# Two-layer decoder on one core: last four chunks and last norm by pairs of blocks, narrower waits, new step orders

## The reference

```
x = layernorm(x + L0_attn(x))    # linear attention, 16 heads, elu + 1
x = layernorm(x + L0_xattn(x))   # 4 experts of token ids: silu(x C) * (x C), times C
x = layernorm(x + L0_ffn(x))     # 8 dense experts, width 256, weights from a sigmoid router, top 2 as a fallback
x = layernorm(x + L1_attn(x))    # 16 heads in groups of 32 tokens, half the heads rolled by 16
x = layernorm(x + L1_xattn(x))   # softmax(x C^T / 16) C under a padding mask
x = layernorm(x + L1_ffn(x))     # 8 experts of width 176, softmax router, top 2, and a shared expert of width 352
# an expert: (silu(x Wg^T) * (x Wu^T)) Wd^T, times its weight
```

## Time and profile before

| | us |
|---|---|
| median of 3 runs | 455.77 (455.28 to 457.13) |
| the profiled execution | 452.04 |
| its span, first to last instruction | 450.2 |
| PE busy / weight loads | 424.8 / 365.9 |
| DVE / ACT / POOL busy | 250.6 / 247.2 / 261.9 |
| transfers | 35.2 MB, 24% of 16 engines' span |

### The profile page before, as it was taken

One profiled execution on the slowest core, in us unless ns is written; L12 is line 12 of the kernel. 1 busy time (PEld: TensorE's weight loads), 2 busy tenths in 40 slices (PEclk: granted clock), 3 DMA queues, 4 the chain that ended last, 5 costly groups with the idle time before them and its releaser, 6 DMA issues.

```text
span 450.2 us, 9291 instructions
## 1 busy us (share of the span) xinstructions
PE 424.8 (94%) x3668; PEld 365.9 (81%) x3668; DVE 250.6 (56%) x627; ACT 247.2 (55%) x424; POOL 261.9 (58%) x217
## 2 busy tenths in 40 slices
PE   7999999999999999999999997799999999999992
PEld 5788889997887887788888986588888888888981
DVE  5568557668437935565354757347435566533233
ACT  4747664773783446518337674454526756565331
POOL 1242753646774897548674663665547574877661
PEclk9999999999999999999999999999999999999996
DMA  8334200021221423312232021232041221433101
GB/s 253 121 92 169 70 1 0 2 70 49 75 90 48 139 75 99 131 49 80 66 95 66 8 76 41 87 85 81 6 149 42 82 81 48 159 126 128 41 1 47
DMA packets 15671, 35.22 MB, mean 78 GB/s; under 512 B 2027, under 2 KB 5995, under 8 KB 15628
## 3 DMA queue, kind: packets, MB, share of 16 engines
q1 hardware_dynamic: 15152, 34.00, 24.1%
q10 hardware_dynamic: 476, 0.63, 0.5%
HBM read 33.05 MB, written 1.05 MB: 76 GB/s over the span
## 4 chain that ended last, share of the span: by engine, by line
PE 50%; DVE 5%; ACT 4%; POOL 4%; issue 2%; DMA 1%; SPq 1%; ACTq 0%; POOLq 0%; DVEq 0%
PE bank L435 9%; PE bank L438 8%; PE bank L436 8%; PE bank L679 5%; PE bank L681 5%; PE bank L680 5%; ACT x_tok L905 2%; DVE stats L1303 2%; PE bank L753 2%; POOL rstd L1158 1%; PE bank L741 1%; DMA state<-o_tok 1%; PE bank L725 1%; PE bank L636 1%; PE bank L727 1%
## 5 line engine op out<-in xcount | busy, mean ns | idle before, releaser
L1192 POOL TENSOR_TENSOR h_lo<-hraw,h_hi 128x512 fp32r<-128x512 f32 x76 | 98.2, 1296 | 60.2 <-ACT h_hi L993 60.0
L435 PE MATMUL bank<-xT_hi,pk_hi 128*128 128x512 f32 x256 | 103.3, 404 | 4.1 <-DVE hraw L1480 3.2
L436 PE MATMUL bank<-xT_hi,pk_lo 128*128 128x512 f32 x256 | 101.6, 397 | 0.7 <-issue 0.7
L993 ACT ACTIVATE h_hi<-hraw 128x512 fp32r<-128x512 f32 x76 | 47.9, 630 | 81.7 <-DVE hraw L1480 75.0
L1198 POOL TENSOR_TENSOR pk_lo<-pk_raw,pk_hi 128x512 fp32r<-128x512 f32 (+1 forms) x44 | 74.7, 1697 | 17.2 <-ACT pk_hi L1011 17.0
L1480 DVE TENSOR_TENSOR hraw<-bank,sil 128x512 f32<-128x512 f32 x76 | 52.3, 688 | 53.7 <-PE bank L438 21.0
L438 PE MATMUL bank<-xT_lo,pk_hi 128*128 128x512 f32 x256 | 80.8, 397 | 0.0
L679 PE MATMUL bank<-pk_hi,h_hi 128*128 128x256 f32 x272 | 78.1, 287 | 2.1 <-DVE x_tok L1494 2.0
L681 PE MATMUL bank<-pk_hi,h_lo 128*128 128x256 f32 x272 | 76.9, 283 | 0.0
L680 PE MATMUL bank<-pk_lo,h_hi 128*128 128x256 f32 x272 | 76.8, 282 | 0.0
L1203 POOL TENSOR_TENSOR pk_lo<-pk_raw,pk_hi 128x256 fp32r<-128x256 f32 (+1 forms) x44 | 42.3, 962 | 34.4 <-ACT pk_hi L1022 34.4
(11 more groups left out here) (245 smaller groups left out, 727.0 us busy)
## 6 DMA issues: line engine op xcount, KB each, us to landing
pk_raw<-pk_f_dram SPq DMA_DIRECT2D x28, 448.0 KB, 3.4
pk_raw<-pk_f_dram SPq DMA_DIRECT2D x16, 512.0 KB, 3.5
pk_raw<-pk_f_dram SPq DMA_DIRECT2D x16, 256.0 KB, 2.7
kv_buf<-pk_x_dram SPq DMA_DIRECT2D x4, 512.0 KB, 3.5
x_tok<-x_rows_dram SPq DMA_DIRECT2D x1, 1024.0 KB, 9.5
pk_raw<-pk_x_dram SPq DMA_DIRECT2D x4, 256.0 KB, 6.4
out_dram<-x_tok SPq DMA_DIRECT2D x4, 256.0 KB, 2.2
kv_buf<-w_attn_dram SPq DMA_DIRECT2D x1, 768.0 KB, 4.4
```

What stands on the lines that cost most here:

```text
L435: pe.matmul(o, w(kc)[0], x(kc)[0], start=kc == 0, stop=False)
L436: pe.matmul(o, w(kc)[1], x(kc)[0], start=False, stop=False)
L993: A(h_hi[:, row, at * 512:(at + 1) * 512], hraw[:, s % 2, :], ACT.Copy).then_inc(sems["hid_hi"], 1)
L1192: pool.tensor_tensor(h_lo[:, row, q], hraw[:, s % 2, :], h_hi[:, row, q].bitcast(F32), ALU.subtract).then_inc(sems["hid_lo"], 1)
```

## The change

- The last four chunks go by pairs of blocks: step `e` is `down` for blocks 0 and 1, `f` for blocks 2 and 3; the order ends `e48 e49 e50 f48 e51 f49 f50 f51`.
- The last norm (11) goes by the same pairs: DVE `w0`, `w1` (addition and statistics of two tiles), POOL `w0`, `w1`, ACT tiles 4 to 6, and DVE tile 7 (`last_apply`); the last store waits for both.
- `gate(s)` for s = 18 to 48 waits for silu of s - 2 alone; the wait for `hid_mul >= s - 1` moves to `up(s)`, between the two products. `up` of an L1 chunk behind a shared chunk waits for silu of s - 2 (`up(49)`: for the multiplication of 46).
- `down(u)`, u below 24, waits for the additions by pairs: blocks 0 and 1 of the unit before ahead of its own blocks 0 and 1, then the others.
- All five orders are new. The diff is cut in the orders, where "..." stands for whole lines of a list, and leaves out the name of the new semaphore.

```diff
 SP_ORDER = """
-G0 D0 G1 D1 S0 G2 D2 G3 D3 G4 D4 G5 D5 G6 D6 G7 D7 G8 D8 G9 D9 G10 D10 G11 D11 S1 G12 S2 S3 D12 G13 D13 G14 D14 R0 G15
-D15 G16 G17 G18 G19 S4 G20 G21 G22 G23 G24 G25 G26 G27 R1 G28 G29 G30 G31 G32 G33 G34 G35 G36 G37 G38 G39 O0 G40 G41
-G42 G43
+G0 D0 G1 D1 S0 G2 S1 D2 G3 D3 G4 D4 G5 D5 G6 D6 G7 D7 G8 D8 G9 D9 G10 D10 G11 S2 S3 D11 G12 D12 G13 D13 G14 D14 R0 G15
+D15 G16 G17 G18 G19 G20 G21 G22 S4 G23 G24 G25 G26 G27 R1 G28 G29 G30 G31 G32 G33 G34 G35 G36 G37 G38 G39 G40 G41 G42
+G43 O0
 """.split()
 PE_ORDER = """
 b0.0 b0.1 b0.2 b0.3 b0.4 b0.5 b0.6 b0.7 b1.0 b0.8 b1.1 b0.9 b1.2 b1.3 b1.4 b1.5 b1.6 b1.7 n0.2 b1.8 g0 g1 b1.9 g2 g3
-d0 g4 n1.2 g5 g6 d1 g7 g8 d2 g9 g10 d3 g11 g12 d4 g13 r0.2 d5 g14 r0.3 g15 g16 u16 d6 g17 d7 u17 g18 u18 g19 u19 d8
-g20 u20 g21 u21 r1.2 d9 r1.3 g22 u22 g23 d10 u23 g24 u24 g25 u25 g26 u26 g27 d11 u27 d12 g28 u28 g29 d13 u29 g30 u30
-g31 u31 d14 d15 g32 u32 g33 u33 a0.2 g34 u34 a0.3 a0.4 d16 a0.5 a0.6 a0.7 g35 a0.8 u35 g36 u36 g37 u37 d17 a0.10 g38
-u38 a0.25 g39 u39 a0.11 d18 a0.26 g40 u40 g41 d19 u41 g42 u42 a0.14 g43 u43 a0.15 g44 d20 a0.16 u44 g45 a0.17 d21
-a0.18 u45 g46 u46 g47 u47 a0.21 d22 a0.22 d23 g48 u48 g49 u49 a1.2 g50 a0.24 a1.3 a1.4 u50 d24 a1.5 a1.6 a1.7 d25 a1.8
-g51 u51 g52 u52 g53 d26 a1.10 u53 a1.25 d27 d28 a1.11 d29 g54 a1.26 u54 g55 u55 g56 u56 g57 u57 a1.14 d30 d31 a1.15
-g58 u58 a1.16 g59 d32 a1.17 u59 a1.18 d33 d34 g60 u60 a1.21 g61 u61 a1.22 g62 u62 g63 d35 d36 d37 a1.24 u63 g64 d38
-u64 g65 d39 u65 g66 d40 u66 g67 u67 g68 d41 u68 g69 d42 d43 u69 g70 u70 g71 u71 g72 u72 d44 d45 d46 d47 g73 u73 g74
-u74 g75 u75 d48 d49 d50 d51
+d0 g4 n1.2 g5 g6 d1 g7 g8 d2 g9 d3 g10 g11 d4 r0.2 g12 g13 r0.3 g14 d5 g15 d6 g16 u16 g17 u17 g18 d7 u18 g19 u19 g20
+u20 g21 d8 u21 r1.2 d9 r1.3 g22 u22 g23 u23 g24 d10 u24 g25 u25 d11 g26 u26 g27 u27 g28 d12 u28 g29 u29 d13 g30 u30
+g31 u31 d14 d15 g32 u32 g33 u33 g34 a0.2 u34 g35 a0.3 a0.4 d16 a0.5 a0.6 a0.7 u35 a0.8 g36 u36 g37 u37 g38 u38 g39
+a0.10 d17 a0.25 d18 a0.11 u39 g40 a0.26 u40 g41 u41 g42 u42 g43 d19 a0.14 u43 a0.15 g44 d20 a0.16 u44 g45 a0.17 u45
+g46 a0.18 d21 u46 g47 u47 a0.21 d22 a0.22 d23 g48 u48 g49 u49 g50 u50 g51 a1.2 d24 d25 a0.24 a1.3 a1.4 d26 u51 a1.5
+a1.6 a1.7 g52 a1.8 d27 u52 g53 u53 g54 d28 a1.10 u54 a1.25 g55 a1.11 u55 a1.26 g56 u56 g57 u57 d29 d30 d31 a1.14 g58
+a1.15 u58 g59 a1.16 u59 g60 a1.17 u60 a1.18 d32 d33 d34 d35 a1.21 g61 u61 g62 a1.22 d36 u62 g63 u63 g64 u64 d37 a1.24
+g65 d38 d39 u65 g66 u66 g67 u67 g68 d40 d41 u68 d42 g69 u69 g70 u70 d43 d44 d45 d46 g71 u71 g72 u72 g73 u73 g74 u74
+g75 u75 d47 e48 e49 e50 f48 e51 f49 f50 f51
 """.split()
 ACT_ORDER = """
-p0 p1 b0.0 b0.1 b0.2 b0.3 p2 p3 p4 X0 X1 b0.8 X2 X3 b1.0 b1.1 b1.2 b1.3 n0.1 n0.2 b1.8 G0 D0 s0 h0 s1 h1 s2 h2 s3 n1.1
...
-a0.14 s42 h42 s43 a0.15 D14 a0.16 h43 s44 h44 a0.17 G15 D15 s45 h45 s46 a0.20 h46 s47 a0.21 h47 G16 D16 G17 D17 a0.22
...
-D34 h64 s65 G35 D35 G36 D36 h65 s66 h66 s67 G37 z0 h67 D37 G38 s68 h68 s69 D38 G39 D39 G40 h69 s70 h70 s71 h71 s72 h72
-D40 G41 D41 G42 D42 s73 G43 D43 h73 s74 h74 s75 h75 z1
+p0 p1 p2 b0.0 b0.1 b0.2 b0.3 p3 p4 b0.8 b1.0 b1.1 X0 X1 X2 X3 b1.2 b1.3 n0.1 n0.2 G0 b1.8 s0 h0 s1 h1 S0 s2 h2 s3 n1.1
...
+h41 s42 h42 s43 a0.15 a0.16 D14 G15 h43 s44 a0.17 h44 s45 h45 s46 D15 G16 a0.20 a0.21 h46 s47 h47 D16 G17 D17 G18
+a0.22 s48 D18 G19 S3 D19 G20 h48 s49 h49 s50 a1.1 a1.2 a0.24 h50 a1.4 S4 s51 D20 G21 D21 G22 D22 h51 s52 h52 a1.9 s53
...
+h64 s65 D34 G35 D35 h65 s66 G36 h66 s67 h67 D36 G37 D37 G38 s68 D38 h68 s69 h69 s70 h70 G39 D39 G40 D40 G41 D41 s71
+G42 D42 h71 s72 G43 h72 s73 z0 h73 s74 h74 s75 D43 h75 z1
 """.split()
 POOL_ORDER = """
-p1 p3 p4 X0 X1 X2 X3 n0.0 v0 G0 D0 l0 l1 n1.0 l2 l3 l4 l5 l6 l7 l8 l9 r0.0 l10 l11 l12 G1 D1 l13 l14 l15 l16 l17 G2
...
-G15 D15 a0.19 l45 l46 l47 G16 D16 G17 a1.0 S3 D17 G18 l48 S4 l49 D18 G19 D19 G20 D20 G21 a1.7 D21 a1.8 l50 l51 l52 l53
...
-l71 D40 G41 D41 G42 D42 G43 D43 l72 l73 l74 l75 y1
+p1 p3 p4 X0 X1 X2 n0.0 X3 v0 G0 l0 l1 n1.0 l2 S0 l3 l4 l5 l6 l7 l8 l9 r0.0 l10 l11 l12 D0 l13 G1 l14 l15 D1 G2 l16
...
+l44 l45 a0.19 D15 G16 l46 l47 D16 G17 D17 G18 D18 G19 a1.0 D19 l48 l49 G20 S3 l50 D20 G21 D21 G22 D22 l51 a1.7 a1.8
...
+G31 l60 l61 D31 G32 D32 G33 l62 l63 D33 G34 l64 D34 G35 D35 l65 G36 l66 D36 G37 D37 G38 D38 l67 l68 l69 l70 G39 D39
+G40 D40 G41 D41 y0 G42 D42 G43 l71 l72 l73 l74 D43 l75 w0 w1
 """.split()
 DVE_ORDER = """
-n1.0 m2 m3 a0 m4 n1.2 m5 m6 a1 m7 m8 a2 m9 m10 a3 r0.0 m11 a4 m12 r0.2 m13 a5 m14 r0.3 m15 r0.4 a6 m16 r0.5 m17 a7 m18
-r1.0 m19 a8 m20 r1.2 a9 m21 r1.3 m22 r1.4 a10 m23 m24 m25 r1.5 a11 m26 m27 a12 c m28 a13 m29 m30 m31 a14 a15 a0.0 m32
-a0.2 m33 a0.3 a0.4 a16 a0.5 a0.6 m34 a0.7 a0.8 m35 m36 a0.9 a0.10 m37 a17 a0.25 m38 m39 a0.11 a0.26 a18 m40 a0.12 m41
-a19 a0.14 m42 a0.15 a20 m43 a0.16 m44 a0.17 a21 a0.18 a0.19 m45 m46 m47 a0.21 a22 a0.22 a23 a0.23 a1.0 m48 a1.2 a1.3
...
-a1.14 o57 m57 a1.15 a1.16 o58 m58 a1.17 o59 m59 a1.18 a1.19 o60 m60 a1.21 o61 m61 a1.22 a1.23 m62 x0 m63 m64 y0 o65
-m65 o66 m66 o67 m67 o68 m68 o69 m69 o70 m70 o71 m71 o72 m72 o73 m73 o74 m74 o75 m75 x1 y1
+n1.0 m2 m3 a0 m4 m5 n1.2 m6 a1 m7 m8 a2 m9 a3 r0.0 m10 a4 m11 r0.2 m12 m13 r0.3 m14 a5 r0.4 m15 a6 r0.5 m16 a7 m17
+r1.0 m18 m19 m20 a8 m21 r1.2 a9 r1.3 m22 m23 r1.4 a10 m24 m25 a11 m26 r1.5 m27 a12 m28 c m29 a13 m30 m31 a14 a15 a0.0
+m32 a0.2 m33 a0.3 m34 a0.4 a0.5 a0.6 a0.7 m35 a0.8 m36 a16 a0.9 m37 m38 a17 a0.10 a0.25 a18 a0.11 m39 a0.26 m40 a0.12
+m41 a19 a0.14 m42 a0.15 m43 a20 a0.16 m44 a0.17 m45 a0.18 a0.19 a21 m46 a0.21 m47 a22 a0.22 a23 a0.23 m48 a1.0 m49 m50
...
+o57 m57 a1.14 a1.15 o58 m58 a1.16 o59 m59 a1.17 o60 m60 a1.18 a1.19 a1.21 o61 m61 a1.22 m62 a1.23 m63 x0 m64 o65 m65
+o66 m66 o67 m67 o68 m68 o69 m69 o70 m70 y0 o71 m71 o72 m72 o73 m73 o74 m74 o75 m75 w0 w1 z1
 """.split()
...
             def store(h):
                 for t in range(0, HT, 2):
                     T = HT * h + t
-                    sp.wait_ge(sems["ln_done"], 4 * (10 + h) + t + 2)
+                    if h and t:
+                        sp.wait_ge(sems["ln_done"], 4 * nth(11) + 3)
+                        sp.wait_ge(sems["last_done"], 1)
+                    else:
+                        sp.wait_ge(sems["ln_done"], 4 * (10 + h) + t + 2)
                     sp.dma_start(out_v[:, T:T + 2, :], x_tok[:, T:T + 2, :]).then_inc(sems["out_done"], 16)
 
             for step in SP_ORDER:
...
                 else:
                     pe.wait_ge(sems["g_lo"], 2 * E0 + u - U_F1 + 1)
                 first = {0: 0, 2 * EX: 1, S_F0: 2, S_F0 + 2 * E0: 3, S_F1: 8, S_F1 + N1: 9}.get(s)
-                if s >= 2:
+                if S_F0 + 2 <= s <= S_F1:
+                    pe.wait_ge(sems["silu_done"], s - 1)
+                elif s >= 2:
                     pe.wait_ge(sems["hid_mul"], s - 1)
                 if u < U_F1:
                     product(s, bank[2 * c][:, :], 0, D, c * P, first).then_inc(sems["gate_ready"], 1)
...
                 if u < U_F0:
                     return
                 if u < U_F1:
+                    pe.wait_ge(sems["hid_mul"], s - 1)
                     product(s, bank[2 * c + 1][:, :], KC * D, D, c * P).then_inc(sems["up_ready"], 1)
                     return
                 m, h = u - U_F1, (u - U_F1) // N1
...
                               cwT[:, h * 512:(h + 1) * 512], start=True, stop=True).then_inc(sems["cw_ready"], 1)
                 if m and routed(m - 1):
                     pe.wait_ge(sems["m1_done"], routed_no(m))
-                else:
-                    pe.wait_ge(sems["hid_mul"], s)
+                elif m == 1:
+                    pe.wait_ge(sems["hid_mul"], S_F1 - 1)
+                else:
+                    pe.wait_ge(sems["silu_done"], s if m == 0 else s - 1)
                 product(s, bank[(3 * m + 2) % 4][:, :], D, P, 0).then_inc(sems["up_ready"], 1)
 
             def open_sums(h):
...
                     pe.matmul(bank[4 + j][:, :], zero_r[:, 0:P], zero_r[:, :], start=True, stop=False,
                               skip_group_check=True)
 
-            def down(u):
+            def down(u, tiles=range(HT)):
                 if u < U_F0:
                     e = u % EX
                     chunks, wh, wl = KC, x0_pack(e, pk_hi, xp_hi), x0_pack(e, pk_lo, xp_lo)
...
                     pe.wait_ge(sems["d_lo"], 2 * E0 + m + 1)
                     chunks, wh, wl = 1, d_part("f1", m, pk_hi), d_part("f1", m, pk_lo)
                 pe.wait_ge(sems["hid_lo"], 2 * (u + 1) if u < U_F1 else S_F1 + u - U_F1 + 1)
-                if 1 <= u < U_F1:
-                    pe.wait_ge(sems["acc_done"], 4 * u)
                 closed = u < U_F1
-                for t in range(HT):
+                for t in tiles:
                     o = bank[4 + t // 2][:, (t % 2) * D:(t % 2 + 1) * D]
+                    if 1 <= u < U_F1 and t % 2 == 0:
+                        pe.wait_ge(sems["acc_done"], 4 * u - 2 + t)
                     for kc in range(chunks):
                         row, at = place(u, kc)
```

(61 more changed lines are left out.)

28 lines of the change are left out of this document (13 added, 15 removed).

## The result

The changed kernel takes 452.82 us (median of 8 executions, 448.86 to 455.45) against 455.52 (8 executions) for the kernel before: ratio 0.9937, with a 95% interval of 0.991 to 0.9963. Measured a second time it was 0.9955 (0.9926 to 0.9983). So it is faster by some 0.6%: 2.9 us by the ratio, 2.7 between the two medians. The forecast was 7.5 us: the sign is right, the size is too large by a factor of 2.6. The median lies just inside the stated range.

What follows compares the result with a forecast made beforehand. PE, busy for 94% of the span, was taken to set the time, so late starts were counted. Terms -2.2 - 1.2 - 1.1 - 0.8 - 4.4 + 0.8 + 1.4 = -7.5 gave 455.8 - 7.5 = 448.3 us, range 444.5 to 453.0.

Steps and rivals of the forecast that it cites:

- Tail: Behind the last matmul: working by pairs shortens the closing additions, norm and store from 6.3 to 4.1 us, -2.2.
- d15: This down step's late start, 1.2 us, goes because its first blocks wait only for the first pair of additions, -1.2.
- d12: This down step's late start, 1.1 us, goes because the additions no longer stand behind the chain r1.5, -1.1.
- g19: This gate's late start, 0.8 us, goes because it waits for silu alone, not a multiplication behind r0.5, -0.8.
- 272 to 288: PE's stretch from 272 to 288 us: new waits and orders leave 2.1 us lost instead of 6.5, -4.4.
- (C): Rival: the change does more, also shortening waits left as they were, with no losses at the start: 445.5 us, chance 0.13.
- What it adds: New delays: +0.8 near the start from later weights and low parts, +1.4 at a0.15 and a1.15 (0.7 each).
- The steps behind them meet as before: 0: Attention steps a0.3, a0.4, a1.3, a1.4 and those behind them meet as before, costing 0.
- (A): Rival: new waits replace old at r0.5, d12 and norm 5, plus 1.5 us of unseen waits: 452.9 us, chance 0.20.
- (B): Rival: slower, as ACT stands at G0 near the start until a slow transfer lands: 455.9 us, chance 0.05.

Runs made afterwards that it cites:

- again_before: The kernel before, unchanged, run again for a second trace: 453.47 us, ratio 0.9982.
- again_after: The changed kernel, run again for a second trace: 452.37 us, ratio 0.9955 to the kernel before.
- e_pool: The changed kernel with POOL's G2 and D1 moved behind l16, so POOL is idle beside most of r0.5: 449.42 us, ratio 0.9893 to the kernel before.
- e_waits: The kernel before, in its own orders, with the change's end by pairs and all its new waits: 453.16 us, ratio 0.9983.
- e_best0: e_pool with G7 ahead of D6 and, on ScalarE, of h27, and on VectorE a1.0 and m48 ahead of a0.23: 453.13 us, ratio 0.997.
- e_best: e_best0 with the first half's context steps spaced apart on PE and l39 ahead of a0.12 on POOL: 450.88 us, ratio 0.9927.
- e_pool_space: e_pool with the first half's context steps spaced apart on PE and l39 ahead of a0.12 on POOL: 448.64 us, ratio 0.9874.
- e_oldwaits: The changed kernel's orders and end by pairs, with the old waits of gate, up and down: 469.36 us, ratio 1.0353 to the kernel before.
- e_tail: The kernel before with only the change's end by pairs of blocks, in its own orders and old waits: 452.13 us, ratio 0.9957.
- e_close: The kernel before with one context step, a0.25, moved directly behind a0.10 on PE: 458.03 us, ratio 1.0109.
- e_space: The changed kernel with the four context steps of each half set further apart in PE's order alone: 453.76 us, ratio 0.9994 to the kernel before.

## Why the prediction was right and wrong

By the second traces (again_before, again_after), and where noted the first.

- **Tail, -2.2**: right, -2.6 (8.9 to 6.3). DVE's tile takes 0.41 us, less than the 0.69 that I took from the nearest row, so ACT's tile of 0.60 ends last; D43 delays nothing. The estimate of 0.2 us from the Trainium skill (VectorE: DVE Perf Modes, "The perf-mode tier table") was too low.
- **d15, -1.2**: right, 0.3 of it is left.
- **d12, -1.1**: the late start is gone, and the sentence behind it, "no other step of PE is due sooner than the waiting ones", is wrong. ScalarE has D6 and G7 behind s28 and h27, h27 behind m27, m27 behind r1.5. G7's low part ends at 158.1 and g30 starts 1.1 late. Net nothing.
- **g19, -0.8**: wrong. The start of r0.5 was right (94.3 forecast, 94.5 measured), its 6.9 us were not: they held for the place where it stood before, with POOL idle beside most of it. In the new place POOL's D1 and G2 fall into it and hold two operations for 3.2 us more than they take (one hold of 1.1, at `none_in`, was within the 6.9, and `zone` takes 0.4 more); it ends at 103.9, and u18 is 2.1 late, +1.3 in place of -0.8. e_pool shows it by giving the time back.
- **272 to 288, -4.4**: nearly right. Of 2.7 at u49, 1.6 for the clock and 1.2 at g50 there remain 0.5 at d23 and 0.9 at g50: -4.1. (Two slips in the sums: a1.3's wait counts as 1.0 before and as 0.8 after, so -4.4 should have been -4.2; and the terms that (C) names add up to 3.0, not 2.8.) The new wait was g50 for m48 behind a0.23, not a1.2. e_waits shows that this gain needed the orders. (In the first trace of after, and in those of e_best0, e_best, e_pool_space and e_oldwaits, the clock falls here at d23 for 3.4 us, 1.7 lost; what sets whether it does I can't say.)
- **What it adds, +0.8 and +1.4**: PE's work up to u18, its first 100 us, came out at -0.2, not +0.8 (0.9 gained at b0, which I had not looked at, and 0.5 lost around b1.9, 0.4 of it at b1.9 itself). a0.15 and a1.15 are 0.7 and 0.3 late, and of 0.5 at a1.18 there remains 0.3: +0.8.
- **"The steps behind them meet as before: 0"**: this is the step that failed most, a term put at nothing. In the two context stretches the stops cost 2.9 us before (1.5, 0.75 and 0.6, no low clock), and after 3.8 (with 0.3 at a smaller one) and half of 3.4 + 6.8 of low clock, 8.9 in all: +6.0. Only 0.9 of it is longer stops; 5.1 is the low clock behind them, which differs from one execution to the next. Between the four steps of the second half lay 1.8, 3.1 and 3.0 us of other work, now 2.2, 1.6 and 1.6. In the first half the time between them is the same, but d17 stands in place of a product, 24 instructions more; the stop there was 1.0 to 2.1 us in five traces with the order before (before, again_before, e_tail, e_waits, e_close), and 1.7 to 2.8 in seven with the new one. No run tests whether these 24 instructions are the reason. I had seen the two issue stops of before and left them out because the profile names no cause.

Sum over the second traces: -2.6 - 0.9 + 0 + 1.3 - 4.1 - 0.2 + 0.8 + 6.0 = +0.3. A wait of 0.9 for low weights at g57 (340.7), which the first trace of before doesn't have and which is gone after, and small places give the rest to the measured -1.2 (451.4 to 450.1). Without the stops' +6.0 it would be -7.2: about the forecast, partly by errors that cancel. That figure is arithmetic and no promise: e_space took the stops away and won nothing. The rival that came nearest is (A), new waits in place of old: r0.5 and d12 did give back what they won. But the mechanism that decided was in no rival, and that (A)'s 452.9 is the measured median is luck; so is it that the median falls inside the range. (B) did not occur: b1.9 is 0.6 late at most in all traces.

Settled: what the stops are, that setting the small-matmul steps closer or further apart makes or removes them (e_close, e_space), and that POOL's work made r0.5 long. Open: how much of what the stops cost could be won back, since e_space and e_pool_space show that a stop is partly cover for the next wait; and when the clock falls behind a stop. In e_pool's trace a stop of 2.3 us had no low clock behind it, in after's one of 2.3 had 6.8 us of it.

## What to carry to other kernels

- A stop called issue is a measurement, not noise: count the engine's instructions up to it. If it recurs at a fixed remainder of 256 and ends soon after a packet of the instruction queue, it is code, and long matmuls between the stretches of short ones remove it (e_space); but the next wait for data can take all that becomes free, so look for that first. At another remainder look for a wait that the profile has no name for: the one at d19 in e_space, at remainder 22, was gone when l39 came earlier (e_best).
- The length of a chain of small VectorE operations is not its own: before it is moved, list what POOL does in the new place; an operation of the chain that begins beside one of POOL can be held to that one's end (2.31 us for 0.19 here).
- Compare medians and the clock of each execution before reading two traces against each other; here the traces had the opposite order of the medians.

## What the runs showed of the hardware

- PE's code arrives in packets of 16 KB, 256 instructions. In the dense stretches the packets start 3.3 to 5.2 us apart, and where PE had stopped, it went on 1.2 to 1.5 us after one had landed. Four steps of 256 instructions in 1.26 us each outran that. The Trainium skill (Runtime: NRT & Kernel Launch, "Instruction fetch mechanics") gives blocks of 16 KiB, 256 instructions, and calls the cost of crossing a border mostly hidden. The traces agree on the blocks; on the cost they don't, it was up to 3.3 us.
- Behind late starts of PE of 1.5 us and more the granted clock was at 0.50 for 3.4, 6.8 or 10.2 us, or stayed at 1.00 (behind 2.3 us at 225 in e_pool). At d23 it fell behind a late start of 0.5 only, in five of the ten traces with the new order. Behind the stop in a0.26 it was low for 6.8 us in after, for 3.4 in again_after and not at all in e_pool, and the time of an execution goes with its mean clock: in again_after 450.7 at 0.995 and 455.0 at 0.978.
